# The destinations of the result rows calculated on VectorE in place of GpSimd

## The reference

```python
def _L0_ffn_ref(x, Wr, br, ln_g, ln_b, W1, b1, W2, b2):
    logits = xt @ Wr + br
    probs = jax.nn.softmax(logits, axis=-1)
    top_p, top_idx = jax.lax.top_k(probs, TOP_K)
    weights = top_p / top_p.sum(axis=-1, keepdims=True)
    ...
    h = jax.nn.gelu(jnp.einsum('end,edh->enh', xe, W1) + b1[:, None, :], approximate=False)
    y = jnp.einsum('enh,ehd->end', h, W2) + b2[:, None, :]
    ...
    out = (weights[:, :, None] * sel).sum(axis=1)

x = x + _L0_conv_ref(_ln_c(x), ...)
t = _to_tokens(x)
t = t + _L0_ffn_ref(_ln_t(t), ...)
```

## Time and profile before

| | |
|---|---|
| median of 3 runs | 2870.46 us (2868.31 to 2876.31) |
| the profiled execution | 2866.05 us, of which the span on the core 2864.3 us |
| busy share of the span | PE 96%, PEld 90%, DVE 80%, ACT 51%, POOL 48% |
| first and last `index` on POOL | 2523.0 and 2806.1 us from the span's start |
| first and last `send` DMA | 2540.3 and 2820.9 us |

### The profile page before, as it was taken

The page is one execution under the profiler, slowest core; times in us unless marked ns, Lnnn a source line. Parts: engine busy times, 40 slices in busy tenths (PEclk is TensorE's granted clock), DMA queues, the critical chain, the costliest instruction groups (busy, mean ns, idle before and its releaser), DMA issues.

```text
span 2864.3 us, 50916 instructions
## 1 busy us (share of the span) xinstructions
PE 2762.0 (96%) x20202; PEld 2592.1 (90%) x20202; DVE 2279.5 (80%) x3471; ACT 1465.8 (51%) x1883; POOL 1388.0 (48%) x1049
## 2 busy tenths in 40 slices
PE   6999999999999999999999999999999999998996
PEld 5899989998999999998999899989999899987786
DVE  6777798778978888878877897889877888866563
ACT  3455445553555345544555355544554455566671
POOL 4344533545445533643355534653364335547783
PEclk9999999999999999999999999999999999999998
DMA  2555030102102121202111210202110211146786
GB/s 110 208 189 222 18 101 23 33 25 96 38 26 72 45 63 43 65 17 100 45 30 56 88 46 25 73 30 78 23 47 10 96 34 31 57 139 216 226 266 213
DMA packets 99794, 238.04 MB, mean 83 GB/s; under 512 B 20088, under 2 KB 24770, under 8 KB 99558
## 3 DMA queue, kind: packets, MB, share of 16 engines
q1 hardware_dynamic: 90470, 217.85, 23.3%
q0 software_dynamic: 9088, 16.94, 1.7%
HBM read 131.23 MB, written 105.30 MB: 83 GB/s over the span
## 4 chain that ended last, share of the span: by engine, by line
PE 72%; DVE 10%; POOL 7%; issue 5%; ACT 4%; DMA 1%; another core or an unknown queue 1%; SPq 0%; POOLq 0%; DVEq 0%; ACTq 0%
PE PV L752 48%; PE MX L752 12%; PE ST L752 11%; POOL yrows L710 3%; DVE E L1566 1%; DVE rt L1571 1%; ACT xr L1217 1%; DVE ul L1525 1%; ACT h L1217 1%; DVE E L1567 1%; POOL acc L639 1%; DVE mcol L1601 1%; DMA y<-yrows 1%; DVE vt L1549 1%
## 5 line engine op out<-in xcount | busy, mean ns | idle before, releaser
L639 POOL TENSOR_TENSOR acc<-acc,tmp 128x256 f32<-128x256 f32 x512 | 803.8, 1570 | 1199.6 <-DVE tmp L1616 1197.6
L1217 ACT ACTIVATE Eh<-ST 128x1024 fp32r<-128x1024 f32 x512 | 525.4, 1026 | 734.8 <-PE ST L752 734.8
L1601 DVE TENSOR_REDUCE mcol<-MX 128x1 fp32r<-128x1024 f32 x512 | 625.5, 1222 | 238.9 <-PE MX L752 238.2
L752 PE MATMUL PV<-vh,Eh 128*128 128x258 f32 x4096 | 766.2, 289 | 0.0
L752 PE MATMUL PV<-vh,El 128*128 128x258 f32 x4096 | 746.1, 284 | 0.0
L752 PE MATMUL PV<-vl,Eh 128*128 128x256 f32 x4096 | 736.2, 281 | 4.4 <-DVE vl L1596 4.4
L752 PEld LDWEIGHTS PV<-vh,Eh 128*128 128x128 f32 x4096 | 631.1, 190 | 50.6 <-issue 6.7
L1606 DVE TENSOR_TENSOR El<-E,Eh 128x1024 fp32r<-128x1024 f32 x512 | 643.4, 1257 | 0.4
L752 PEld LDWEIGHTS PV<-vl,Eh 128*128 128x128 f32 x4096 | 597.7, 189 | 6.1 <-DVE vl L1596 6.1
L752 PEld LDWEIGHTS PV<-vh,El 128*128 128x128 f32 x4096 | 596.8, 190 | 0.0
L1217 ACT ACTIVATE E<-ST 128x1024 f32<-128x1024 f32 x512 | 521.3, 1018 | 0.0
(11 more groups left out here) (264 smaller groups left out, 3340.7 us busy)
## 6 DMA issues: line engine op xcount, KB each, us to landing
rows<-xr SPq DMA_DIRECT2D x68, 520.0 KB, 6.2
stk<-rt SPq DMA_DIRECT2D x64, 512.0 KB, 2.8
kst<-stk SPq DMA_DIRECT2D x192, 128.0 KB
qst<-stk SPq DMA_DIRECT2D x192, 128.0 KB
wt<-wall SPq DMA_DIRECT2D x39, 514.0 KB
wt<-wall SPq DMA_DIRECT2D x39, 512.5 KB
xrow<-rows SPq DMA_DIRECT2D x39, 260.0 KB
y<-yrows SPq DMA_DIRECT2D x32, 256.0 KB, 4.6
```

Of the source, the lines that this page charges most:

```text
L639: nc.gpsimd.tensor_tensor(acc[:, ic, :], acc[:, ic, :], tmp[:, p, :], ALU.add).then_inc(s_acc, 1)
L752: return nc.tensor.matmul(o, w, m, start=start, stop=stop)
L1217: return nc.scalar.activation(o, i, func, **kw)
L1601: nc.vector.tensor_reduce(mcol[:, k % 2, p:p + 1], MX[:, :], AX, ALU.max).then_inc(s_red, 1)
```

## The change

`index` moves from POOL's list to DVE's, with the same waits and the same arithmetic. On POOL it stood two tiles ahead of `send`. On DVE tiles 0 and 1 stand ahead of the tile loop, and `index(j + 2)` stands behind the first routing piece of turn j, ahead of `gelu_lo(j + 1, 0)`.

```diff
 @block.gpsimd
-            def index(j):
-                wait(pool, t_x[j % XR], 16 * (j // XR + 1))
-                if j >= XR:
-                    wait(pool, t_sc[(j - XR) % YR], 64 * ((j - XR) // YR + 1))
-                nc.gpsimd.tensor_scalar(idx[j % XR][:, :], xrow[j % XR][:, :, C], -1.0, float(2 * NTOK),
-                                        ALU.mult, ALU.add).then_inc(t_ix, 1)
...
-            index(0)
-            index(1)
             for j in range(NT):
-                if j + 2 < NT:
-                    index(j + 2)
                 if j == PAIRED:
...
 @block.vector
+            def index(j):
+                wait(dve, t_x[j % XR], 16 * (j // XR + 1))
+                if j >= XR:
+                    wait(dve, t_sc[(j - XR) % YR], 64 * ((j - XR) // YR + 1))
+                ts(idx[j % XR][:, :], xrow[j % XR][:, :, C], -1.0, float(2 * NTOK), ALU.mult, ALU.add).then_inc(t_ix, 1)
...
             gelu_lo(0, 0)
             gelu_lo(0, 1)
+            index(0)
+            index(1)
             for j in range(NT):
                 if j + 2 < NT:
                     split2(j + 2)
                 between(j, "split")
+                if j + 2 < NT:
+                    index(j + 2)
                 if j + 1 < NT:
                     gelu_lo(j + 1, 0)
```

## The result

The change makes the kernel slower: 2889.76 us (median of 6 runs, 2883.37 to 2893.86) against 2870.84 for the kernel before beside it (2866.04 to 2876.31); ratio 1.0056, 95% interval 1.0043 to 1.0069. The prediction said 2870.2, the same time, with a range up to 2880. The profiled execution took 2885.82 us, its span is 2884.1, 19.8 more than before.

What follows compares the result with a forecast made beforehand. PE was taken to set the steady pace, with POOL or DVE on the path only at a few places; -0.9 + 0.3 + 0.35 = -0.25 us on the profiled execution, on the median 2870.2 us, range 2858 to 2880.

Steps and rivals of the forecast that it cites:

- Taken from POOL, steady part: About 0.6 us a tile leaves POOL's list; worth nothing, since PE sets the pace and POOL will wait for yrow.
- The faster rival: Stall at 2605 to 2665 us comes from POOL's crowded list; half regained gives 2860.2, all 2850; chance 0.18.
- the stretch in doubt: 2605 to 2665 us, among POOL's scatters: PE busy only 45.6 of 60 us, ACT's waits without a named releaser.
- The slower rival: Tiles 8 to 10: DVE's index waits for send 10's landing, holding DVE and PE 10.4 us; 2880.9; chance 0.15.
- Added to DVE: 39 index calculations of 128x4 on DVE, 0.17 us each where POOL rests, 0.35 where it issues; hidden in steady part.
- A calculation stands behind a POOL DMA: Each DVE index waits for a running POOL DMA, costing up to 1.87 + 0.17 us; 2871.8; chance 0.05.
- The end: Last tiles: POOL's sends are the path and start less late behind yrow; -0.9 us (-1.46 to 0).
- The start: Indexes of tiles 0 and 1 on DVE delay the first El that PE waits for; +0.3 us (0.3 to 1.2).
- The turn of tile 10: One index on DVE ahead of both hl of tile 11, where DVE has no slack; +0.35 us (0.17 to 0.6).
- What would show it wrong: PE busy much more or less than 45.6 of the 60 us behind 2605, or DVE's idx waiting for a DMA.

Runs made afterwards that it cites:

- e1: The change plus one POOL instruction without use ahead of each tile's sends, where index stood; 2871.58 us, ratio 0.9992.
- e9: The kernel before plus four further indirect DMAs of 128 rows behind each send of tiles 3 to 6; 2883.87 us, ratio 1.0059.
- e13: The kernel before plus 16 POOL additions of 128x192, and no additional DMAs, in tiles 3 to 6; 2881.12 us, ratio 1.0031.
- e3: The kernel before with the last batch's 16 scatters issued two behind each send of tiles 8 to 15; 2874.25 us, ratio 1.0000.
- e7: The change plus two spare POOL instructions a tile, ahead of the sends and between second and third DMA; 2877.36 us, ratio 1.0034.
- e4: The change with each tile's second to fourth send held back by waits for steps of DVE; 2881.95 us, ratio 1.0026.
- e5: The change plus a spare POOL instruction ahead of every other tile's sends only; 2870.66 us, ratio 1.0009.
- e6: The change plus a spare POOL instruction between the second and third DMA of each tile's send; 2868.71 us, ratio 1.0005.
- e14: The kernel before plus 16 indirect DMAs in tiles 3 to 6 that each move one row; 2886.57 us, ratio 1.0055.
- e8: The change without SP's loads of the experts' weights from tile 2 on; 2876.23 us, ratio 1.0023.
- e11: The change plus a spare POOL instruction ahead of every tile's sends and a second inside those of tiles 8 to 15; 2867.92 us, ratio 1.0006.

## Why the prediction was wrong

- *Taken from POOL, steady part:* **the step that failed.** It read that PE waits for none of POOL's list, and therefore priced the 0.6 us a tile that leave the list at nothing. It cost 14.3 us between tiles 20 and 38, because what went was the pause between POOL's DMAs: e1, with another instruction in that place, takes 116.4 us there, the change 130.1, the kernel before 115.8. That PE did not wait for POOL was true of the list as it stood.
- *The faster rival* had the right mechanism and the wrong sign. It took the late signals for POOL's doing, as e9 against e13 shows for tiles 3 to 6 and e3 makes likely for the scatters, but counted six indexes as crowd. Without them the stretch in doubt stayed as it was (tiles 8 to 20: 102.0 us, then 100.2); in the steady part the indexes were the gaps, and the same trouble came there. The earlier trace rows showed that a quarter of PE's time can be at stake where POOL's DMAs come close (14.4 of 60 us), and the prediction priced that for one stretch and one sign only.
- *The slower rival*, DVE behind a send that has not landed, did not happen with the change (it did in other runs, most of all in e7): in the view of groups `idx` has no idle time before it (the last number; busy us and mean ns ahead of it).

```profile
L1999 DVE TENSOR_SCALAR idx<-xrow 128x4 uint32<-128x4 f32 x39 | 9.9, 257 | 0.0
```

- *Added to DVE:* right. 0.15 to 0.37 us each, and DVE has idle time for them. *A calculation stands behind a POOL DMA:* given 0.05, and it did not happen; none took the 0.97 us of a DMA. The rule of the Trainium skill, SBUF — State Buffer, section Who interferes with whom, that the later one fully blocks, is stated for a calculation in a two-port mode; these rows show no such wait, but they don't show the mode either, so they don't decide on the rule.
- *The end:* right. The last send starts 8.50 us behind the end of the last `yrow` (before 9.57, from 2811.31 to 2820.88), a gain of 1.1 where 0.9 was forecast. It is lost again ahead of that: with the late signals of the last tiles (ACT's `yev` at 2817.71 waits 2.92 us) the way from tile 38 to the end is 3.1 us longer. DVE's timeline before, then POOL's and DVE's after:

```profile
2810.62 0.69 DVE L2011 TENSOR_TENSOR yrow<-PV,xrow 128x512 f32<-128x512 f32 x1 [3.47 <-PE PV L1145]
```

```profile
2841.35 0.97 POOL L703 DMA_INDIRECT yrows<-yrow,idx  x1 [0.30 <-issue]
```

```profile
2832.16 0.69 DVE L2006 TENSOR_TENSOR yrow<-PV,xrow 128x512 f32<-128x512 f32 x1 [4.14 <-PE PV L1134]
```

- *The start:* PE's wait for the first `El` is 1.84 us (1.70 in the earlier trace rows), 0.1 more where 0.3 was forecast:

```profile
2533.66 0.66 PE L904 MATMUL MX<-ident,acc 128*128 128x128 f32 x4 [1.84 <-DVE El L1969]
```

- *The turn of tile 10:* smaller than forecast. From the start of `r_list` to that of the `hl` behind it are 0.16 us (2612.43 to 2612.59), before 0.09 (2608.79 to 2608.88), where 0.35 more was forecast, and PE doesn't wait there.
- *What would show it wrong* named the stretch behind 2605 and DVE's waits, and neither showed it. What failed was a sign listed as showing it right, a PE busy throughout the steady part. POOL's idle gap ahead of the sends came as said, but in the steady part ahead of every third tile's only.

## What to carry to other kernels

An engine that issues indirect DMAs can slow the whole core without being waited for: before work is taken out from between such DMAs, look at how far apart they are and whether any stretch of the trace, with DMAs closer together, already shows waits without a named releaser. A wait that the profile can't attribute is a mechanism not yet understood, and its price belongs into the range with both signs. Here pauses made by waits vanished when the engine was behind (e4); work as a pause stayed (e1). And a whole time that comes back can hide a loss that has only moved (e5, e6): compare stretch by stretch.

## What the runs showed of the hardware

Indirect DMAs that POOL issues one right behind the other make the signals of PE late, by 3.2 us at 2704 in the change and with 11.3 us of idle ACT in e9, while PE's records run on until PE itself needs what is waiting, and ACT's signal at 2708.89 comes at once. It happens whether the DMAs move 128 rows or one (e9, e14), and with the DMA engines busy a third of the time (e8). Late signals stood behind rows of twelve without a pause (their starts 1.44 us apart on the mean, in the change), of seven with one index between (1.42, the scatters before) and of eight with one index between (1.38, e9); in the steady stretch before, four and an index at 6.47 us a tile had none. The distance alone does not decide: over the 40 DMAs of tiles 8 to 13 it is 1.51 us in e1, where ACT's `yev` waits up to 11.5 us, and 1.51 in e11, with one late signal (1.5 us).

Behind an idle stretch PE had a lower clock: 0.80 on the mean in e9's stretch, where it had stood 11 us idle up to 2596.63; that is for part of the stretch the lower level of 1.2 GHz. In the same stretch before it was 1.00 (2.4 GHz). Twelve sends in a row at the very end, 2806.76 to 2821.85 before, have no late signal that can be seen; PE's tiles are nearly over there. By what way POOL's issuing holds up PE's signals no run shows; that stays open.
